# Turned softmax blocks of a four-head attention step, carried through HBM in one piece or as two head pairs

## The reference

```python
q = _rope(_rmsnorm(q, q_norm_w), pos); k = _rope(_rmsnorm(k, k_norm_w), pos)
k_all = jnp.concatenate([kc, k], axis=1); v_all = jnp.concatenate([vc, v], axis=1)
scores = jnp.einsum('bqhd,bkhd->bhqk', q, k_all) * SCALE
scores = jnp.where(valid[:, None, None, :], scores, -1e+30)
probs = jax.nn.softmax(scores, axis=-1)
o = jnp.einsum('bhqk,bkhd->bqhd', probs, v_all)
return jnp.einsum('bse,de->bsd', o.reshape(bsz, seqlen, HQ * D), Wo)
```

## Time and profile before

| | us |
|---|---|
| median of 3 runs | 1224.59 |
| lowest and highest | 1222.09, 1231.84 |
| profiled execution | 1230.89 |
| its span, first to last instruction | 1229.2 |
| PE busy | 1139.0 (93%) |
| DVE busy | 850.5 (69%) |
| ACT busy | 683.5 (56%) |
| POOL busy | 475.6 (39%) |
| mean granted clock of PE | 0.985 |
| packets of SP's DMA queue, share of 16 engines' span | 61.3% |

### The profile page before, as it was taken

One profiled execution on the slowest core, in us unless ns is written; L12 is line 12 of the kernel. 1 busy time (PEld: TensorE's weight loads), 2 busy tenths in 40 slices (PEclk: granted clock), 3 DMA queues, 4 the chain that ended last, 5 costly groups with the idle time before them and its releaser, 6 DMA issues.

```text
span 1229.2 us, 27100 instructions
## 1 busy us (share of the span) xinstructions
PE 1139.0 (93%) x6112; PEld 979.4 (80%) x6112; DVE 850.5 (69%) x2167; ACT 683.5 (56%) x1914; POOL 475.6 (39%) x570
## 2 busy tenths in 40 slices
PE   5998789999999999999999999999999999999986
PEld 3555678888888888888888888888888888888874
DVE  2335667777777777777777777776777777777671
ACT  2223556665565665565666565665656665566550
POOL 6752334444333343333444333343333443232310
PEclk8999799999999999999999999999999999999998
DMA  5573477777777787777777777787777777767764
GB/s 171 189 273 133 136 229 231 241 236 226 238 242 242 245 252 230 228 247 240 240 239 227 233 249 238 241 255 229 218 243 237 249 226 221 233 215 227 241 197 137
DMA packets 83690, 277.31 MB, mean 226 GB/s; under 512 B 12633, under 2 KB 12761, under 8 KB 74459
## 3 DMA queue, kind: packets, MB, share of 16 engines
q1 hardware_dynamic: 71368, 236.23, 61.3%
q0 software_dynamic: 11152, 36.72, 10.1%
q10 hardware_dynamic: 1154, 4.19, 0.9%
HBM read 186.92 MB, written 90.18 MB: 225 GB/s over the span
## 4 chain that ended last, share of the span: by engine, by line
PE 50%; DMA 30%; DVE 7%; issue 6%; SPq 5%; ACT 1%; DVEq 0%; POOL 0%; POOLq 0%; ACTq 0%
DMA blocks_placed<-blocks 15%; DMA prob_t<-blocks_placed 13%; PE ps_o L911 12%; PE ps_q L848 8%; SPq L364 4%; PE ps_kv L848 4%; DVE blocks L1152 3%; PE ps_s L748 3%; PE ps_s L750 3%; PE ps_s L749 3%; PE ps_x L750 2%; PE ps_x L748 2%; DVE kt_lo L1055 2%; PE ps_x L749 2%; PE ps_l L780 2%
## 5 line engine op out<-in xcount | busy, mean ns | idle before, releaser
L911 PE MATMUL ps_o<-prob_t,v_raw 128*128 128x256 f32 x1024 | 251.5, 390 | 57.9 <-DMA prob_t<-blocks_placed 53.6
L685 ACT ACTIVATE prob<-prob,low 128x640 f32<-128x640 f32 x256 | 210.1, 825 | 126.8 <-DVE low L1134 117.3
L911 PEld LDWEIGHTS ps_o<-prob_t,v_raw 128*128 128x128 f32 x1024 | 193.9, 194 | 90.5 <-issue 60.5
L1134 DVE CUSTOM_DVE_ANT_0 prob<-ps_s,mask,q_gain 128x640 f32<-128x640 f32 x256 | 215.7, 880 | 35.6 <-PE ps_s L750 35.6
L1152 DVE STREAM_TRANSPOSE blocks<-prob 128x640 f32<-128x640 f32 x256 | 214.0, 837 | 0.4 <-ACT prob L690 0.2
L690 ACT ACTIVATE prob<-prob,inv 128x640 f32<-128x640 f32 x256 | 196.7, 817 | 0.6 <-DVE inv L1140 0.6
L638 ACT ACTIVATE ot_hi<-ps_o 128x256 fp32r<-128x256 f32 x128 | 49.2, 384 | 241.3 <-PE ps_o L911 241.3
L748 PE MATMUL ps_s<-kt_hi,qt_hi 128*128 (+2 forms) x512 | 172.0, 336 | 5.2 <-DVE kt_lo L1055 3.7
L848 PE MATMUL ps_q<-w_hi,x_s 128*128 (+1 forms) x512 | 172.6, 397 | 0.0
L750 PE MATMUL ps_s<-kt_hi,qt_lo 128*128 (+2 forms) x512 | 160.3, 313 | 0.0
L749 PE MATMUL ps_s<-kt_lo,qt_hi 128*128 (+2 forms) x512 | 160.0, 313 | 0.0
(11 more groups left out here) (138 smaller groups left out, 2212.0 us busy)
## 6 DMA issues: line engine op xcount, KB each, us to landing
blocks_placed<-blocks SPq DMA_DIRECT2D x256, 320.0 KB
prob_t<-blocks_placed SPq DMA_DIRECT2D x64, 1280.0 KB
x_s<-xt_split SPq DMA_DIRECT2D x64, 512.0 KB
w_raw<-w_qkvo_dram SPq DMA_DIRECT2D x55, 320.0 KB
w<-w_t_dram SPq DMA_DIRECT2D x8, 1024.0 KB, 5.8
xt_split<-x3t ACTq DMA_DIRECT2D x8, 512.0 KB
w_raw<-w_qkvo_dram POOLq DMA_DIRECT2D x9, 320.0 KB, 5.7
xbt<-x_t_dram SPq DMA_DIRECT2D x8, 256.0 KB, 2.7
```

The lines of the kernel that those rows point to most:

```text
L685: nc.scalar.activation(prob[:, h, :], prob[:, h, :], ACT.Exp, bias=low[:, h:h + 1], scale=-1.0, accum_out=total[:, h:h + 1]).then_inc(exp_ ...
L911: mm = nc.tensor.matmul(ps_o[pair][:, 0:PAIR], v, turned_probs(c, pair), start=c == 0, stop=c == CH - 1)
L1134: nc.vector.tensor_tensor_reduce(out=prob[:, h, :], in0=ps_s[:, score_slot(h):score_slot(h) + KEYS], in1=mask[:, :], scale=q_gain[:, h:h + ...
```

## The change

The tile `blocks`, the HBM scratch and the tile `prob_t` each get an outer dimension for the head pair. `place_blocks` is called twice in a step, with a pair: each call waits for the two heads of its pair, scatters 4 times 160 KB in runs of 1,280 bytes (`RUN` is 320 floats), waits for these four on a semaphore of the pair, waits for the pair's own values of the unit before, and loads 640 KB into the pair's half of `prob_t`. PE waits for `pt_in[0]` before pair 0 and for `pt_in[1]` before pair 1. DVE's heads 0 and 2 each wait for the scatter of their own pair. What each compute instruction computes, and how many there are, stays as it was. In the changed file the line numbers of `place_blocks` are one higher, those of PE and DVE two.

```diff
+RUN = CH * GROUP // 2 * BLOCK
...
-        blocks_dram = nc.dram_tensor("blocks_placed", [NB, BLOCK, NB, CH * GROUP * BLOCK], F32).ap()
+        blocks_dram = nc.dram_tensor("blocks_placed", [2, NB, BLOCK, NB, RUN], F32).ap()
...
-            blocks = sb("blocks", [P, NB, CH, GROUP, BLOCK], scope=p2)
-            prob_t = sb("prob_t", [P, NB * CH * GROUP * BLOCK], scope=p2)
+            blocks = sb("blocks", [P, 2, NB, CH, GROUP // 2, BLOCK], scope=p2)
+            prob_t = sb("prob_t", [P, 2, NB * RUN], scope=p2)
...
-                return prob_t[:, :].rearrange("p (a c h q) -> p h a c q", a=NB, c=CH, h=GROUP)[:, 2 * pair:2 * pair + 2, :, c, :]
+                return prob_t[:, pair, :].rearrange("p (a c h q) -> p h a c q", a=NB, c=CH, h=GROUP // 2)[:, :, :, c, :]
...
-                    def place_blocks(n, first=False):
+                    def place_blocks(n, pair, first=False):
 
-                        sp.wait_ge(blocks_turned, GROUP * (n + 1))
+                        sp.wait_ge(blocks_turned, GROUP * n + 2 * pair + 2)
                         sp.nop(nofuse=True)
                         if not first:
-                            sp.wait_ge(pt_in, 16 * n)
+                            sp.wait_ge(pt_in[pair], 16 * n)
                             sp.nop(nofuse=True)
                         for a in range(NB):
-                            sp.dma_start(blocks_dram[:, :, a, :].rearrange("j i r -> i j r"),
-                                         blocks[a * BLOCK:(a + 1) * BLOCK, :, :, :, :].rearrange("p j c h q -> p j (c h q)")).then_inc(blocks_out, 16)
-                        sp.wait_ge(blocks_out, 16 * NB * (n + 1))
+                            sp.dma_start(blocks_dram[pair, :, :, a, :].rearrange("j i r -> i j r"),
+                                         blocks[a * BLOCK:(a + 1) * BLOCK, pair, :, :, :, :].rearrange("p j c h q -> p j (c h q)")).then_inc(blocks_out[pair], 16)
+                        sp.wait_ge(blocks_out[pair], 16 * NB * (n + 1))
                         sp.nop(nofuse=True)
                         if not first:
-                            sp.wait_ge(pv_done, 2 * n)
+                            sp.wait_ge(pv_done, 2 * (n - 1) + pair + 1)
                             sp.nop(nofuse=True)
-                        sp.dma_start(prob_t[:, :], blocks_dram.rearrange("j i a r -> (j i) (a r)")).then_inc(pt_in, 16)
+                        sp.dma_start(prob_t[:, pair, :], blocks_dram[pair].rearrange("j i a r -> (j i) (a r)")).then_inc(pt_in[pair], 16)
...
-                        place_blocks(n, first)
+                        place_blocks(n, 0, first)
+                        place_blocks(n, 1, first)
...
-                        pe.wait_ge(pt_in, 16 * (u + 1))
                         if not first:
                             pe.wait_ge(ot_lo_out, 2 * u)
                         for pair in (0, 1):
+                            pe.wait_ge(pt_in[pair], 16 * (u + 1))
...
-                        if h == 0 and not first:
-                            dve.wait_ge(blocks_out, 16 * NB * n)
-                        nc.vector.transpose(blocks[:, :, :, h, :].rearrange("p j c q -> p c j q"),
+                        if h % 2 == 0 and not first:
+                            dve.wait_ge(blocks_out[h // 2], 16 * NB * n)
+                        nc.vector.transpose(blocks[:, h // 2, :, :, h % 2, :].rearrange("p j c q -> p c j q"),
```

More of the change, by code:

```diff
@@ L245, in build @@
             blocks_turned = psem("blocks_turned")
-            blocks_out, pt_in = psem("blocks_out"), psem("pt_in")
+            blocks_out, pt_in = [psem(f"blocks_out_{pair}") for pair in (0, 1)], [psem(f"pt_in_{pair}") for pair in (0, 1)]
             pv_done, ot_hi_out, ot_lo_out = psem("pv_done"), psem("ot_hi_out"), psem("ot_lo_out")
@@ L1183, in step @@
                             cached_low(n + 1, ps_o1)
-                        turn_blocks(n, 2)
+                        turn_blocks(n, 2, first)
                         if not last:
```

## The result

| | before | changed |
|---|---|---|
| median of the runs, us | 1228.21 (4 runs) | 1254.59 (4 runs) |
| lowest and highest | 1222.09, 1232.41 | 1249.17, 1261.53 |
| profiled execution | 1230.89 | 1255.85 |
| mean step, unit 0 to unit 61 | 16.88 | 17.33 |
| packets of both main DMA queues, share of the span | 71.4% | 69.1% |

The changed kernel is slower: ratio 1.0222, 95% interval 1.0148 to 1.0296, which lies wholly above 1. The forecast was 1160, with a range of 1152 to 1198. A fourth run of the kernel before moved its median from 1224.59 to 1228.21. The mean step is (1210.84 - 153.54) / 61 = 17.33 us from the values of unit 0 to those of unit 61, taken as before in the earlier trace rows; 61 x 0.45 = 27 us cover the 26 us between the medians.

What follows compares the result with a forecast made beforehand. PE's own work was taken as the bound, 15.91 us a step once its waits for prob_t go. Saving 59.3 us over 61 steps and 5.0 at the end, 64.3 from 1224.6, gave 1160 us, range 1152 to 1198.

Steps and rivals of the forecast that it cites:

- What bounds the kernel: Main loop: PE's own work takes 15.91 us a step; every second step PE also waits for prob_t, 53.6 us in all.
- Price of short runs: Scatters to blocks_placed: a 1,280-byte run takes 96 ns if rate limits, 192 if all is per packet.
- Rival 1: SP's queue: both pairs' round trips fill it, slower if a run exceeds 139 ns; 1276 us at 153 ns; chance 0.07.
- The sequence on SP: SP's scatters and loads: pair 0 lands at V + 7.7, pair 1 at V + 14.7, so PE never waits.
- V: On PE: the start of a unit's values, the zero from which the forecast's times in a step are counted.
- 2D + 8.0: SP's closed cycle from scatter to scatter in us, D being a pair's scatter data time, 3.1; together 14.2.
- DMA has room: DMA queues in the main loop: busy share of 25.5 us in two steps, 12.8 of 15.9 in one.
- Rival 3: PE's values: PE waits as before, now at pair 1, so no change; 1215 to 1235 us; chance 0.03.

Runs made afterwards that it cites:

- e2: Changed kernel with one 1,280 KB load for both pairs, pair 0 scattered after head 1 and pair 1 after head 3; 1163.7 us, ratio 0.9485.
- e3: Changed kernel with both pairs' scatters issued ahead of both loads; 1160.8 us, ratio 0.9445.
- e6: Changed kernel with x_s and w_raw reloaded for 16 of 128 partitions only, a timing test; 1162.6 us, ratio 0.9485.
- e9: e3 with the scatters in the order of partition groups 0, 2, 1, 3; 1160.0 us, ratio 0.9451.
- e5: Kernel before with an extra wait on SP: groups 0 and 1 must land before 2 and 3 are scattered; 1290.1 us, ratio 1.0514.
- e7: Kernel before with a unit's four scatters in the order of partition groups 0, 2, 1, 3; 1194.4 us, ratio 0.9746.
- e8: Changed kernel with each pair's four scatters in the order of partition groups 0, 2, 1, 3; 1254.0 us, ratio 1.0234.
- e1: Changed layout (1,280-byte runs, eight scatters) in the order of the kernel before: all scatters after head 3, one load; 1211.1 us, ratio 0.9854.

## Why the prediction was wrong, point by point

**What bounds the kernel: right.** PE's own step without a wait is 15.91 us; e2, e3, e6 and e9 run at 15.86. Their 1160 to 1164 us are the forecast's number, of another kernel.

**Price of short runs: no one number, and not what failed.** I took 96 ns, with 192 as the bad bound. e6 has 93, where the scatters have little ahead of them; the changed kernel has 57 in the middle of a scatter that stood behind 1.5 MB. I had set 56 aside as a gain without a reason. A reason may be that the scatters of both sides of SBUF then overlap, which isn't shown. Rival 1 came true in its result (the two round trips fill SP's queue, the kernel is slower), but not by its price: its point of decision, a run over 139 ns, was never near.

**The sequence on SP: the step that failed.** "Pair 0: issued V - 1.0, done V + 3.8", 5.0 us to the load's issue; it takes 8.1, and in the step shown none of its runs moves in the first four. Everything else in the cycle was about right: 6.4 predicted and 6.37 measured for pair 1; 0.6 and 0.57; 2.2 and 2.34 for the other issues. For pair 1 part of this is luck: its runs move at 367 GB/s in 619.5:621, about 61 ns each, so its data is 1.1 us shorter than I had it, and something I didn't tell apart takes that time instead. I charged pair 1's scatter for the load queued ahead of it, and didn't charge pair 0's for the three that stand ahead of it: pair 1's load of 0.66 MB, `x_s` and `w_raw`. In my sequence they were to be over. The closed cycle of rival 1, 2D + 8.0, left them out as well, although it was to describe a queue that is never idle. With 8.1 in it, it is 17.3, over PE's 15.9. e6 puts 2.4 of the 3.1 us on `x_s` and `w_raw`; the rest is the load of pair 1, the only thing left ahead in e6, or the end of the scatter, which wasn't tried apart. The split is rough, since the scatter's own runs move at 206 GB/s there and at 376 in the changed kernel. The changed kernel's last steps say the same as e6: where `w_raw` is no longer loaded pair 0 takes 7.4 us (8 steps), and 5.6 and 6.4 in the last two, without `x_s` too, though a store of the output stands ahead in some of them.

The start of the loop shows that it isn't a matter of a lucky start. SP's queue, unit 0 and 1:

```profile
137.19 2.05 SPq L365 DMA_DIRECT2D blocks_placed<-blocks  x4
143.47 0.34 SPq L372 DMA_DIRECT2D prob_t<-blocks_placed  x1
143.91 2.26 SPq L365 DMA_DIRECT2D blocks_placed<-blocks  x4
150.40 0.34 SPq L372 DMA_DIRECT2D prob_t<-blocks_placed  x1
151.21 0.36 SPq L350 DMA_DIRECT2D x_s<-xt_split  x1
151.90 0.35 SPq L355 DMA_DIRECT2D w_raw<-w_qkvo_dram  x1
152.79 2.15 SPq L365 DMA_DIRECT2D blocks_placed<-blocks  x4
160.87 0.34 SPq L372 DMA_DIRECT2D prob_t<-blocks_placed  x1
```

Unit 1's pair 0 is issued 0.75 us before PE's values of unit 0 at 153.54, nearly where the plan had it (V - 1.0), and already takes 8.08 us: 1.5 MB were put on the queue in the 2.4 us ahead of it.

**"DMA has room": true and beside the point.** The busy share was 12.8 of 15.9 us by my count, and is 12.0 of 17.33 now (69.1%). What counts is that a handshake leaves the engines idle; e5 puts one at about 1.4 us of the round trip. Before, SP's queue had room for its one handshake: it stood 358 us waiting for turned blocks, and PE waited for `prob_t` only in every second step. The change adds a second handshake, and the queue then has no idle time of its own.

**Rival 3** (PE waits at pair 1) describes what PE sees: it waits there 60 times in 64 units, and not once at pair 0. Its time, 1215 to 1235, was too low. I held it for unlikely, because I looked at pair 1's landing and not at SP's next pass.

## What to carry to other kernels

When a transfer is split to start earlier, write down the issuing queue's whole pass as a closed cycle, with every transfer's data charged to whatever stands behind it, and compare it with the bound engine's step. A second blocking wait in an in-order queue can take more than the earlier start gives; issue all the scatters first and wait afterwards, which here made the same split 5.5% faster than before instead of 2.2% slower.

## What the runs showed of the hardware

- The order of four scatters out of 32-partition groups is worth 2.5% (e7): 238 GB/s in the order 0, 2, 1, 3 and 213 in the order 0, 1, 2, 3. In the changed kernel the same order gains nothing (e8).
- The layout with runs of 1,280 bytes cost no more DMA time than that with 2,560 for the same bytes: 755 and 754 us of mean engine time in e1 and before. What one such run takes depends on what the queue holds: 93 ns in e6, 57 in the changed kernel.
- A transfer waits for the data queued ahead of it: pair 0's scatter took 8.1 us behind 1.5 MB, 5.7 with 0.75 MB of that taken away (e6), and pair 1's took 4.2 with no load issued between the pairs (e2).
- One more handshake between dependent transfers costs about 1.4 us of a round trip (e5). In the changed kernel nearly nothing moves around one, between 639 and 641, though the mean share is 69%.
